# Cutting the normalisation of attention products into two pieces on VectorE, and moving the query projection one slot ahead

## The chip, the cores and the metric

One core of a Trainium2 chip. The metric is the device time of one execution in microseconds. The kernel before took 652.82 us, the median of three runs (652.71 to 653.96).

## The reference, cut to what matters

A batch of 8 images goes through two convolution blocks and then, as 256 tokens of 256 channels per image, through two attention layers with a small linear layer behind each. The change lies in the attention layers. For each of 16 heads of 16 dimensions:

```python
scores = q @ k.T / sqrt(dh) (+ bias in the first layer), masked causally
attn   = softmax(scores)
out    = (attn @ v)  -> (B, L, D)
t      = t + out @ w_out (+ b_out)
```

The softmax is not normalised where it is computed: the exponentials are multiplied with v and with a column of ones, and the product is divided by that column's result afterwards. The first attention layer (stage 0) is followed by a matrix product with ternary weights (stage 1), the second (stage 2) by a mixture of 8 experts, of which 2 count for each token (stage 3).

## The kernel before, in words

**Bodies and slots.** After the convolutions the work is 16 bodies: body 0 to 7 is stage 0 for image 0 to 7, body 8 to 15 is stage 2 for image 0 to 7. Each body starts 12 slots after the one before it (`BODY = 12`). A body is cut into pieces, each with a step; the slot of a piece is 12 times the body's number plus its step. `in_order` (L142) sorts all pieces of all bodies by slot, and each engine walks through that list in order. There are two lists: one for TensorE, and one for VectorE (DVE), ScalarE (ACT), GpSimd (POOL) and the DMA queue of SyncE (SP). Within a slot the scores and their maxima (S, MS, M) come first in the second list, then the long readings of slots before (V, PR, FF, E), then the pieces of `attention` (X, O0, O1, ON), then the pieces of `FLOW`; of those the ones of the later body come first. In any stretch of 12 slots pieces of several bodies are mixed. Below, "slot k" counts within the 12.

**The pieces, by the slot of a regular stretch in which they stand before the change.**

- S (12 per body, slots 0 to 11): a matmul of scores on TensorE; VectorE takes the negated row maximum (L1465). MS (L1474, L1475): VectorE splits a group's maxima into two bf16 parts; M (L1251): TensorE turns them, and ScalarE copies them beside the queries (L1361).
- X (12 per body, 6 slots behind S): scores again, transposed and with the maximum taken off (L1262, L1266); ScalarE takes the exponential into a ring of 9 (L1367).
- O0, O1 (L1278, L1285): products with v for the four groups of heads, pair 0 in slot 1 and pair 1 in slot 7, into PSUM bank 7.
- ON (L1476): for each pair, VectorE transposes the products (L1478, `by_token`), takes the reciprocals of the sums (L1481, `oinv`), multiplies (L1482, `attn`) and transposes back (L1486, `attnT`). Pair 0 stands in slot 2 of the next body's stretch, pair 1 in slot 8.
- PR (slot 10, L1203 with `wo`): the output projection of the body before, on TensorE; it waits for `attn_ready` of pair 1. VectorE adds the old tokens (L1495).
- LNa, LNb (stage 0 or 2, for the body two ahead: slots 3 and 5): VectorE's statistics (L1410 to L1416), GpSimd's power (L1147), VectorE's normalisation (L1421, `xn`). T (slot 6): TensorE transposes `xn` (L1187 with `fix,xn`), ScalarE copies it out (L1332). Q (slot 8) and K (slot 9): projections of the body two ahead (L1195); ScalarE writes the first bf16 part (L1346, L1349), VectorE the rest (L1431, L1434). SPLIT: GpSimd makes the second and third part, and SP stores them; in slot 9 for Q and 10 for K. LOAD (SP): slots 0 and 1 of the next stretch. V (slot 10, L1203 with `wt`), read by VectorE (L1456, L1458).
- For the layer behind the attention: LNa, LNb in slots 0 and 1, T in slot 3 (stage 1) or 2 (stage 3), FF (stage 1) or R, RT (router, stage 3), GT (slot 7), GB (slot 8: TensorE L1310, VectorE's `acc` L1538), E (8 expert products, slots 11 to 6, L1316; VectorE accumulates, L1548), CT (slot 8: transposes `acc` for the output, L1187 with `fix,acc`). GB's instruction on VectorE first waits for CT of the image before, which reads `acc`.

**Banks.** Every matmul piece but O0 and O1 takes one of 7 PSUM banks in turn (`RING = 7`), so that a piece waits on TensorE until what was 7 pieces earlier has been read out.

**Waits on VectorE's own results.** `settle` (L1394) increments `dve_step` and lets VectorE wait for it before the next instruction; ON settles the reciprocal and the product (`SETTLED`, L165).

Of the kernel before, what the change touches and what calls it, by code (L numbers as in the profile page):

```python
# [22 lines left out]
PAD = IMG + 2  # L23
HEADS, DH = 16, 16
GROUPS = 4
# [48 lines left out]
PT_RING = 9  # L74
STACKS = 3
LAG = 6
PARTS_OF_MAX = 2

Q_PARTS = (0, 0, 1, 1, 0, 2)
K_PARTS = (0, 1, 0, 1, 2, 0)  # L80
STACK = DH * len(Q_PARTS)
MAX_ROWS = PARTS_OF_MAX * HEADS // GROUPS
MAX_AT, BIAS_AT = STACK, STACK + MAX_ROWS
# [16 lines left out]
def attention():  # L100

    out = [("S", u, u) for u in range(UNITS)]
    out += [("MS", g, 3 * g + 2) for g in range(GROUPS)]
    out += [("M", g, 3 * g + 4) for g in range(GROUPS)]
    out += [("X", u, u + LAG) for u in range(UNITS)]
    for g in range(GROUPS):
        last = 3 * (g | 1) + LAG
        out += [("O0", g, last + 4), ("O1", g, last + 4)]
        if g % 2:
            out.append(("ON", g // 2, last + 5))  # L110
    return out


LONG = ("V", "PR", "FF", "E")

FLOW = {
    0: (("LNa", 0, 0, -21), ("LNb", 0, 0, -19), ("XB", 0, 0, -17), ("T", 0, 0, -18), ("Q", 0, 0, -16),
        ("SPLIT", 0, 0, -15), ("K", 0, 0, -15), ("SPLIT", 0, 1, -14), ("V", 0, 0, -14), ("LOAD", 0, 0, -12),
        ("LOAD", 0, 1, -11), ("PR", 0, 0, 22), ("LNa", 1, 0, 24), ("LNb", 1, 0, 25),
        ("T", 1, 0, 27), ("FF", 1, 0, 29)),  # L120
    2: (("LNa", 2, 0, -21), ("LNb", 2, 0, -19), ("T", 2, 0, -18), ("Q", 2, 0, -16),
        ("SPLIT", 2, 0, -15), ("K", 2, 0, -15), ("SPLIT", 2, 1, -14), ("V", 2, 0, -14), ("LOAD", 2, 0, -12),
# [39 lines left out]

JOBS = ("S", "M", "X", "T", "Q", "K", "V", "PR", "FF", "R", "GT", "GB", "E", "CT")

SETTLED = {"LNa": 2, "MS": 1, "ON": 2, "R": 1, "RT": 3, "E": 1}  # L165


def settled(piece):
    return SETTLED.get(piece[0], 0) + (piece[0] == "RT" and piece[3] == 3)


def signals(piece, bank):

    kind, n = piece[0], piece[3]
    out = []
    if kind in JOBS:
        out += [(f"bank_full{bank}", 1), (f"bank_drained{bank}", 1)]
    if kind == "O1":
        out.append((f"bank_full{PRODUCTS}", 1))
    if kind in SETTLED:  # L180
        out.append(("dve_step", settled(piece)))
    out += {"LNa": [("var_ready", 1), ("rstd_ready", 1)], "LNb": [("xn_ready", 1)], "XB": [("x_biased", 1)],
            "MS": [("max_split", 1)], "ON": [("products_taken", 1), ("attn_ready", 1)], "PAD": [("own_rows", 1), ("padded", 4), ("chosen", 1), ("chosen_spread", 16 * (STACKS - 1))], "CT": [("out_stored", 16)],
            "Q": [("first_ready0", 1)], "K": [("first_ready1", 1)],
            "SPLIT": [(f"second_ready{n}", 1), (f"third_ready{n}", 1), (f"parts_stored{n}", 16)],
            "LOAD": [(f"stack_loaded{n}", 16 * (len(Q_PARTS) + (piece[1] == 0 and n == 0)))],
            "R": [("router_shifted", 1)], "RT": {0: [("router_exp", 1)], 3: [("gates_ready", 1)]}.get(n, [])}.get(kind, [])
    return out


class Counts:


    def __init__(self):
        self.bank, self.after, self.total = {}, {}, {}
        jobs = 0
        for p in in_order("tensor"):
            if p[0] in JOBS:
                self.bank[p] = jobs % RING
                jobs += 1  # L200
            self.add(p, [(name, k) for name, k in signals(p, self.bank.get(p)) if name.startswith("bank")])
        for p in in_order("others"):
            self.add(p, [(name, k) for name, k in signals(p, self.bank.get(p)) if not name.startswith("bank")])
# [10 lines left out]
def build(nc, x_in, fix_in, fixb_in, bias_in, w0_in, w1_in, wt_in, wm_in, parts_dram, out):  # L214
    ctx = ExitStack()
    with ctx:
# [3 lines left out]
        def sem(name):  # L220
            return ctx.enter_context(nc.semaphore(name))
# [13 lines left out]
        def FB(name, lo=0, n=None):  # L235
            at, w = FIXB[name]
            return fixb[:, at + lo:at + lo + (w - lo if n is None else n)]
# [771 lines left out]
        with ExitStack() as c2:  # L1009
            def lb(name, shape, dt=F32):  # L1010
                return sb(name, shape, dt, c2)
# [10 lines left out]
            V = lb("V", [P, STACKS, 2, HEADS, SLOT])  # L1022
# [3 lines left out]
            by_token = lb("by_token", [P, 2, PIX // SLOT, SLOT])  # L1026
            chosen = lb("chosen", [P, HEADS // GROUPS], BF16)
            oinv = lb("oinv", [P, 2, PIX // SLOT])
# [9 lines left out]
            sems = {name: sem(name) for name in COUNTS.total}  # L1038
# [4 lines left out]
            def wait(eng, name, piece, less=0):  # L1043

                value = COUNTS.after.get((piece, name)) if piece else None
                if value is not None and value - less > asked.get((id(eng), name), 0):
                    asked[id(eng), name] = value - less
                    eng.wait_ge(sems[name], value - less)
# [7 lines left out]
            def full(eng, piece):  # L1056

                wait(eng, f"bank_full{bank_number(piece)}", piece)
# [26 lines left out]
            def previous(kind, stage, batch, n, by=1):  # L1085

                at = body(stage, batch) - by
                if at < 0:
                    return None
                s, b = BODIES[at]  # L1090
                return kind, s + stage % 2, b, n
# [5 lines left out]
            def earlier_unit(kind, stage, batch, n, by, per):  # L1097

                return previous(kind, stage, batch, (n - by) % per, (by - n + per - 1) // per)
# [74 lines left out]
            def tensor_piece(pe, piece):  # L1174
                kind, stage, batch, n = piece
# [23 lines left out]
                def toks(w, wstep, w_at, src, width=CH):  # L1199

                    for t in range(2):
                        for c in range(NC2):
                            mm = pe.matmul(d[:, t * width:(t + 1) * width], src[:, c, t * P:(t + 1) * P],  # L1203
                                           w[:, c * wstep + w_at:c * wstep + w_at + width],
                                           start=(c == 0), stop=(c == 1))
                    return mm
# [13 lines left out]
                if kind == "S":  # L1220
# [12 lines left out]
                    g, part = n // 3, n % 3  # L1233
# [19 lines left out]
                if kind == "X":  # L1253

                    g, part = n // 3, n % 3
# [31 lines left out]
                                       start=False, stop=True, skip_group_check=True)  # L1287
                    mm.then_inc(sems[f"bank_full{PRODUCTS}"], 1)
                if kind == "PR":
                    wait(pe, "attn_ready", ("ON", stage, batch, GROUPS // 2 - 1))  # L1290
                    if piece == ("PR", *BODIES[0], 0):
                        pe.wait_ge(wo_loaded, 16 * 2 * (HEADS // GROUPS))
                    mm = toks(wo[:, stage // 2], CH, 0, attnT)
# [95 lines left out]
            def vector_piece(dve, piece):  # L1389
                kind, stage, batch, n = piece  # L1390
# [3 lines left out]
                def settle(ins):  # L1394

                    local[0] += 1
                    ins.then_inc(sems["dve_step"], 1)
                    wait(dve, "dve_step", piece, settled(piece) - local[0])
# [39 lines left out]
                if kind == "PAD":  # L1438
                    dve.wait_ge(fixb_loaded, 16)
                    rows = slice(MAX_AT, MAX_AT + MAX_ROWS)  # L1440
                    half = MAX_ROWS // PARTS_OF_MAX
                    dve.tensor_tensor(chosen[rows, :], FB("ident", MAX_AT, half)[rows, :],
# [17 lines left out]
                if kind == "S":  # L1460
                    full(dve, piece)
                    g, part = n // 3, n % 3
# [5 lines left out]
                if kind == "MS":  # L1468
# [3 lines left out]
                    full(dve, earlier_unit("M", stage, batch, n, 2, GROUPS))  # L1472
                    first, second = (nparts[:, n % 2, :, MAX_AT + 4 * r:MAX_AT + 4 * r + 4] for r in range(PARTS_OF_MAX))
                    settle(dve.tensor_copy(first, nmax[:, par, n]))  # L1474
                    dve.tensor_tensor(second, nmax[:, par, n], first, ALU.subtract).then_inc(sems["max_split"], 1)  # L1475
                if kind == "ON":  # L1476
                    full(dve, ("O1", stage, batch, 2 * n + 1))
                    dve.transpose(by_token[:].rearrange("p g m s -> p (g m s)"), ps[:, PRODUCTS, :])\  # L1478
                       .then_inc(sems["products_taken"], 1)
                    wait(dve, "products_taken", piece)  # L1480
                    settle(dve.reciprocal(oinv[:], by_token[:, :, :, DH]))  # L1481
                    settle(dve.tensor_tensor(attn[:].rearrange("p m g d -> p g m d"), by_token[:, :, :, 0:DH],  # L1482
                                             oinv[:].unsqueeze(3).broadcast_to([P, 2, PIX // SLOT, DH]), ALU.mult))
                    if n == 0:
                        full(dve, previous("PR", stage, batch, 0))
                    dve.transpose(attnT[:, n, :], attn[:].rearrange("p m g d -> p (m g d)"))\  # L1486
                       .then_inc(sems["attn_ready"], 1)
# [11 lines left out]
                L, D, C, one, two, E = (lg[:, k] for k in range(6))  # L1499
# [211 lines left out]
```

## Time and profile before

| | us |
|---|---|
| three timed runs | 652.71, 653.96, 652.82 (median 652.82) |
| the profiled execution | 654.44 |
| its span in the trace | 652.6 |
| TensorE (matmul) busy | 571.2, 88% of the span |
| VectorE busy | 471.1, 72% |
| ScalarE busy | 300.2, 46% |

The convolutions take the first 130 us, the 16 bodies the rest. A stretch of 12 slots takes about 25.6 us while stage 0 runs and about 37.8 us in stage 2. An engine's busy time is the union of its instructions; a matmul's end is modelled, so neighbouring matmuls overlap in the rows. Behind a row, "[idle before <-releaser]" is how long the engine had stood still, and what ended that.

### The profile page before, as it was taken

How to read it: one execution, taken by the hardware profiler on the slowest of the kernel's cores; microseconds unless marked ns; L12 is line 12 of the kernel's file. 1: busy time of each engine (PE TensorE's matmuls, PEld its weight loads, DVE VectorE, ACT ScalarE, POOL GpSimd, SP SyncE). 2: the span in 40 equal slices, each digit the busy share in tenths (PEclk: the TensorE clock that was granted, in tenths of full speed). 3: DMA queues.
4: the chain of work that ended last, by engine and by line, in shares of the span. 5: the costliest groups of instructions: out<-in, count | busy, mean ns of one | idle time of the engine just before them, and what ended most of it. 6: DMA issues, size and time to landing. Idle time of an engine off the chain costs nothing.

```text
span 652.6 us, 10840 instructions
## 1 busy us (share of the span) xinstructions
PE 571.2 (88%) x3994; PEld 385.6 (59%) x4032; DVE 471.1 (72%) x1273; ACT 300.2 (46%) x472; POOL 117.5 (18%) x115
## 2 busy tenths in 40 slices
PE   9875776857988989889889897999999999999997
PEld 3743334745666757757667665657575666555443
DVE  4677858747587687786776876686868768786764
ACT  2356677626455555554545544334343434343110
POOL 2121000351213413313122031203020110000000
PEclk9996998979899999999999997999999999999999
DMA  9700000574224044053142240404113050000000
GB/s 336 256 1 1 1 0 8 136 214 119 66 85 150 27 125 125 31 145 102 46 146 74 74 146 0 146 2 127 37 53 110 16 146 1 17 5 14 17 18 16
DMA packets 40636, 51.15 MB, mean 78 GB/s; under 512 B 4180, under 2 KB 33620, under 8 KB 40276
## 3 DMA queue, kind: packets, MB, share of 16 engines
q1 hardware_dynamic: 40584, 50.46, 25.5%
q8 instruction: 32, 0.52, 0.3%
q14 instruction: 20, 0.16, 0.1%
HBM read 35.63 MB, written 14.68 MB: 77 GB/s over the span
## 4 chain that ended last, share of the span: by engine, by line
PE 50%; DVE 25%; issue 3%; DMA 2%; SPq 1%; ACT 1%; POOL 1%; DVEq 0%; ACTq 0%
PE ps L1316 13%; PE ps L1203 8%; DVE nmax L1465 7%; PE ps L1195 7%; PE ps L1278 4%; PE ps L1266 3%; PE ps L1246 3%; DVE xn L1421 2%; PE ps L1187 2%; DVE acc L1548 2%; PE ps L1262 2%; DVE stats L1410 2%; PE ps L1285 2%; PE ps L1241 2%; DVE by_token L1478 1%
## 5 line engine op out<-in xcount | busy, mean ns | idle before, releaser
L1367 ACT ACTIVATE PT<-ps 128x512 f32<-128x512 f32 x192 | 113.9, 597 | 152.0 <-PE ps L1266 150.5
L1465 DVE TENSOR_REDUCE nmax<-ps 128x2 f32<-128x512 f32 (+1 forms) x192 | 129.7, 683 | 73.3 <-PE ps L1246 70.7
L1316 PE MATMUL ps<-wm,xnT 128*128 128x512 f32 x256 | 120.2, 600 | 0.5 <-DVE acc L1548 0.5
L1361 ACT ACTIVATE QS<-ps 8x1024 bf16<-8x1024 f32 x64 | 65.0, 1016 | 28.9 <-PE ps L1251 27.9
L1266 PE MATMUL ps<-QS,KS 110*128 110x256 bf16 (+3 forms) x512 | 74.5, 247 | 0.0
L1262 PE MATMUL ps<-fixb 128*128 128x256 bf16 (+1 forms) x192 | 60.0, 313 | 16.0 <-DVE nmax L1465 11.3
L1548 DVE SCALAR_TENSOR_TENSOR acc<-ps,gate,acc 128x256 f32<-128x256 f32 x128 | 61.5, 481 | 16.6 <-PE ps L1316 14.3
L1147 POOL TENSOR_TENSOR rstd<-ve,fix 128x2 f32<-128x2 f32 x31 | 21.5, 693 | 258.4 <-DVE ve L1416 258.4
L1316 PEld LDWEIGHTS ps<-wm,xnT 128*128 128x128 f32 x256 | 44.6, 190 | 39.4 <-issue 38.0
L1195 PE MATMUL ps<-xnT,by_dim 128*128 128x256 f32 x256 | 61.0, 383 | 2.2 <-ACT xnT L1332 2.2
L1167 POOL TENSOR_TENSOR parts<-rest,fix 128x512 bf16<-128x512 f32 x30 | 38.0, 1267 | 135.0 <-DVE rest L1434 96.7
L1266 PEld LDWEIGHTS ps<-QS,KS 110*128 110x128 bf16 (+1 forms) x512 | 45.2, 98 | 12.0 <-issue 1.7
L1195 PEld LDWEIGHTS ps<-xnT,by_dim 128*128 128x128 f32 x256 | 46.3, 190 | 8.2 <-ACT xnT L1332 1.8
L1246 PE MATMUL ps<-KS,QS 110*128 110x256 bf16 (+1 forms) x256 | 50.5, 279 | 0.0
L1203 PE MATMUL ps<-wt,xnT 128*128 128x256 f32 x192 | 45.8, 381 | 0.0
L1278 PE MATMUL ps<-PT,V 128*32 128x256 f32 x512 | 41.9, 401 | 0.0
L1203 PEld LDWEIGHTS ps<-wt,xnT 128*128 128x128 f32 x192 | 34.8, 190 | 4.1
L1241 PE MATMUL ps<-fixb 128*128 128x256 bf16 x128 | 35.9, 281 | 1.3 <-DVE rest L1431 1.3
L1171 POOL TENSOR_TENSOR parts<-rest,parts 128x512 bf16<-128x512 f32 x30 | 34.7, 1156 | 2.4
L1246 PEld LDWEIGHTS ps<-KS,QS 110*128 110x128 bf16 (+1 forms) x256 | 25.8, 101 | 14.3 <-issue 8.3
L1187 PE MATMUL ps<-fix,xn 128*128 128x128 f32 x128 | 20.9, 288 | 13.0 <-DVE xn L1421 11.3
L1262 PEld LDWEIGHTS ps<-fixb 128*128 128x128 bf16 x192 | 18.8, 98 | 22.3 <-DVE nmax L1465 13.8
(217 smaller groups left out, 878.3 us busy)
## 6 DMA issues: line engine op xcount, KB each, us to landing
parts_dram<-parts SPq DMA_DIRECT2D x32, 384.0 KB, 3.1
QS<-parts_dram SPq DMA_DIRECT2D x96, 128.0 KB
KS<-parts_dram SPq DMA_DIRECT2D x96, 128.0 KB, 2.7
wt<-wt_dram SPq DMA_DIRECT2D x1, 2562.0 KB, 21.0
wm<-wm_dram SPq DMA_DIRECT2D x1, 2449.0 KB, 13.0
xc<-x_dram SPq DMA_DIRECT2D x8, 256.0 KB, 5.4
out_dram<-res SPq DMA_DIRECT2D x8, 256.0 KB, 2.1
w<-w_dram SPq DMA_DIRECT2D x1, 845.0 KB, 7.6
```

The costliest lines, as they stand in the source:

```text
L1195: mm = pe.matmul(d[:, o * PIX:(o + 1) * PIX], w[:, c, o], src[:, c, :], start=(c == 0), stop=(c == 1))
L1203: mm = pe.matmul(d[:, t * width:(t + 1) * width], src[:, c, t * P:(t + 1) * P], w[:, c * wstep + w_at:c * wstep + w_at + width], start=(c ...
L1241: pe.matmul(d.rearrange("p (j k n) -> p j k n", j=2, k=2)[:, :, 1, :], FB("ident"), FB("tri1").rearrange("p (j n) -> p j n", j=2), start=T ...
L1246: mm = pe.matmul(d[:, jj * PIX:(jj + 1) * PIX], QS[r, at, h, P:2 * P], KS[r, at, h, :], start=False, stop=(jj == 1), skip_group_check=True)
L1262: pe.matmul(d.rearrange("p (j n) -> p j n", n=width)[:, :, 0:P], FB("tri0", 0, P), FB("ident").unsqueeze(1).broadcast_to([P, len(heads), P ...
L1266: mm = pe.matmul(d[:, k * width:(k + 1) * width], KS[r, at, 4 * g + j, kt * P:(kt + 1) * P], QS[r, at, 4 * g + j, kt * P:], start=False, s ...
L1278: pe.matmul(o[32 * j:32 * j + 32, 0:PIX], V[:, at, 0, 4 * n + j, :], PT[:, pt_slot(piece, 3 * n + j // 2), (j % 2) * PIX:(j % 2 + 1) * PIX ...
L1316: mm = pe.matmul(d, normT(stage, batch)[:, c, t * P:(t + 1) * P], M("We", c * EXPERTS * CH + e * 2 * CH, 2 * CH), start=(c == 0), stop=(c ...
L1361: act.activation(QS[MAX_AT:MAX_AT + MAX_ROWS, stack(stage, batch), 4 * n:4 * n + 4, :], bank(piece)[MAX_AT:MAX_AT + MAX_ROWS, 0:PIX].unsqu ...
L1367: act.activation(PT[:, pt_slot(piece, n), :], bank(piece), ACT.Exp).then_inc(drain(piece), 1)
L1465: dve.tensor_reduce(group[:, 0, :] if part == 0 else group[:, 1, 2 * part - 2:2 * part], bank(piece).rearrange("p (j n) -> p j n", n=w_), ...
L1548: op = dve.scalar_tensor_tensor(acc[:, t, :], bank(piece)[:, k * CH:(k + 1) * CH], gate[:, par, t, 2 * e + k:2 * e + k + 1], acc[:, t, :], ...
```

## The change

ON keeps the first transposition and the reciprocals. The product and the transposition back become a piece AT of their own, two slots behind ON for pair 0 (slot 2 to 4) and one slot behind it for pair 1 (slot 8 to 9). The reciprocals now count on a semaphore of their own, on which AT waits. Q goes from slot 8 to 7, its SPLIT from 9 to 8; K stays.

```diff
+TURN_BACK = (7, 6)
...
         if g % 2:
-            out.append(("ON", g // 2, last + 5))
+            out += [("ON", g // 2, last + 5), ("AT", g // 2, last + TURN_BACK[g // 2])]
...
-    0: (... ("Q", 0, 0, -16),
-        ("SPLIT", 0, 0, -15), ("K", 0, 0, -15), ...
+    0: (... ("Q", 0, 0, -17),
+        ("SPLIT", 0, 0, -16), ("K", 0, 0, -15), ...
...
-    2: (... ("Q", 2, 0, -16),
-        ("SPLIT", 2, 0, -15), ("K", 2, 0, -15), ...
+    2: (... ("Q", 2, 0, -17),
+        ("SPLIT", 2, 0, -16), ("K", 2, 0, -15), ...
...
-SETTLED = {"LNa": 2, "MS": 1, "ON": 2, "R": 1, "RT": 3, "E": 1}
+SETTLED = {"LNa": 2, "MS": 1, "AT": 1, "R": 1, "RT": 3, "E": 1}
...
-            "ON": [("products_taken", 1), ("attn_ready", 1)]
+            "ON": [("products_taken", 1), ("inverse_ready", 1)], "AT": [("attn_ready", 1)]
...
                 if kind == "PR":
-                    wait(pe, "attn_ready", ("ON", stage, batch, GROUPS // 2 - 1))
+                    wait(pe, "attn_ready", ("AT", stage, batch, GROUPS // 2 - 1))
...
                     wait(dve, "products_taken", piece)
-                    settle(dve.reciprocal(oinv[:], by_token[:, :, :, DH]))
+                    dve.reciprocal(oinv[:], by_token[:, :, :, DH]).then_inc(sems["inverse_ready"], 1)
+                if kind == "AT":
+                    wait(dve, "inverse_ready", ("ON", stage, batch, n))
                     settle(dve.tensor_tensor(attn[:].rearrange("p m g d -> p g m d"), by_token[:, :, :, 0:DH],
```

By the sorting rule VectorE's order in a regular stretch becomes: slot 2: S, MS, ON (pair 0); slot 3: S, LNa; slot 4: S, AT (pair 0); slot 5: S, MS, LNb; slot 7: S, Q; slot 8: S, MS, ON (pair 1), GB where there is one; slot 9: S, AT (pair 1), K; slot 10: S. TensorE's order becomes, from slot 7: S, M, X, O0, O1, Q, GT, S, X, GB, CT, S, X, K, S, M, X, V, PR. Bodies 14 and 15 have no Q, K and V beside them (there is no body two ahead), and behind body 15's scores there is no S either: VectorE's order at the end is ON (pair 1), GB, AT (pair 1).

## Rows read from the trace of the kernel before

**Rows 1.** By stretch: length, busy PE, PEld, DVE, ACT, POOL; granted clock, DMA, GB/s.

```profile
240.60:266.21 25.61, 22.78 (x207) 17.27 (x209) 19.32 (x54) 13.94 (x23) 7.50 (x7) 1.00 0.32 95
...
391.50:396.10 4.60, 0.76 (x8) 0.32 (x5) 4.08 (x19) 2.81 (x5) 0.69 (x1) 0.95 0.00 1
396.10:402.50 6.40, 6.35 (x49) 4.08 (x50) 2.41 (x9) 2.59 (x4) 0.00 (x0) 0.50 0.00 0
```

**Rows 2.** What TensorE waited for, 170 to 380 us: total, times, longest.

```profile
PE ps L1262 <- DVE nmax L1465: 11.3, 8, 1.4
PE ps L1187 <- DVE xn L1421: 2.5, 8, 0.3
```

**Rows 3.** The chain that ended last, one regular stretch: start, us, what.

```profile
253.22 0.70 DVE nmax L1465
...
266.21 0.66 PE ps L1187 x4
...
278.83 0.70 DVE nmax L1465
```

**Rows 4.** Timeline of VectorE around ON of pair 0: start, us, instruction.

```profile
209.68 0.25 DVE L1481 RECIPROCAL oinv<-by_token 128x16 f32<-128x16 f32 x1
209.96 0.42 DVE L1482 TENSOR_TENSOR attn<-by_token,oinv 128x256 f32<-128x256 f32 x1
210.42 0.45 DVE L1486 STREAM_TRANSPOSE attnT<-attn 128x256 f32<-128x256 f32 x1
210.79 0.65 DVE L1465 TENSOR_REDUCE nmax<-ps 128x4 f32<-128x512 f32 x1
...
212.50 1.28 DVE L1465 TENSOR_REDUCE nmax<-ps 128x2 f32<-128x512 f32 x2
```

**Rows 5.** Timeline of TensorE: T of body 3 and of body 15.

```profile
160.99 1.09 PE L1187 MATMUL ps<-fix,xn 128*128 128x128 f32 x4 [2.85 <-DVE xn L1421]
...
510.43 0.63 PE L1187 MATMUL ps<-fix,xn 128*128 128x128 f32 x4 [0.62 <-DVE xn L1421]
```

**Rows 6.** Timeline, slots 8 to 10 of one stretch: S, Q, its readings, PR.

```profile
217.79 0.28 PE L1241 MATMUL ps<-fixb 128*128 128x256 bf16 x1
...
218.33 0.69 DVE L1465 TENSOR_REDUCE nmax<-ps 128x2 f32<-128x512 f32 x1 [1.60 <-PE ps L1246]
...
218.57 1.95 PE L1195 MATMUL ps<-xnT,by_dim 128*128 128x256 f32 x8
...
220.56 0.84 ACT L1346 ACTIVATE parts<-ps,qk_bias 128x256 bf16<-128x256 f32 x2 [1.19 <-PE ps L1195]
...
221.43 0.88 DVE L1431 SCALAR_TENSOR_TENSOR rest<-ps,qk_bias,parts 128x256 f32<-128x256 f32 x2
...
225.36 1.89 PE L1203 MATMUL ps<-wo,attnT 128*128 128x256 f32 x8
```

**Rows 7.** Timeline of TensorE: expert products, right behind O1 and behind T.

```profile
419.67 1.98 PE L1316 MATMUL ps<-wm,xnT 128*128 128x512 f32 x4
...
422.71 1.88 PE L1316 MATMUL ps<-wm,xnT 128*128 128x512 f32 x4
```

**Rows 8.** Timeline: ON of pair 1 of body 13, GB, PR.

```profile
553.82 0.25 DVE L1481 RECIPROCAL oinv<-by_token 128x16 f32<-128x16 f32 x1
...
554.94 0.65 DVE L1538 TENSOR_TENSOR acc<-ps,xt 128x512 f32<-128x512 f32 x1
...
555.64 1.99 PE L1203 MATMUL ps<-wo,attnT 128*128 128x256 f32 x8 [0.44 <-DVE acc L1538]
```

**Rows 9.** Timeline of the end: ON of pair 1 of body 15, GB, PR.

```profile
611.50 0.25 DVE L1481 RECIPROCAL oinv<-by_token 128x16 f32<-128x16 f32 x1
...
613.27 0.69 DVE L1538 TENSOR_TENSOR acc<-ps,xt 128x512 f32<-128x512 f32 x1 [0.57 <-PE ps L1187]
...
613.00 1.89 PE L1203 MATMUL ps<-wo,attnT 128*128 128x256 f32 x8
```

**Rows 10.** The chain that ended last, behind PR of body 15.

```profile
614.89 1.73 PE ps L1316 x4
```

More of the change, by code:

```diff
@@ L116 @@
 FLOW = {
-    0: (("LNa", 0, 0, -21), ("LNb", 0, 0, -19), ("XB", 0, 0, -17), ("T", 0, 0, -18), ("Q", 0, 0, -16),
-        ("SPLIT", 0, 0, -15), ("K", 0, 0, -15), ("SPLIT", 0, 1, -14), ("V", 0, 0, -14), ("LOAD", 0, 0, -12),
+    0: (("LNa", 0, 0, -21), ("LNb", 0, 0, -19), ("XB", 0, 0, -17), ("T", 0, 0, -18), ("Q", 0, 0, -17),
+        ("SPLIT", 0, 0, -16), ("K", 0, 0, -15), ("SPLIT", 0, 1, -14), ("V", 0, 0, -14), ("LOAD", 0, 0, -12),
         ("LOAD", 0, 1, -11), ("PR", 0, 0, 22), ("LNa", 1, 0, 24), ("LNb", 1, 0, 25),
         ("T", 1, 0, 27), ("FF", 1, 0, 29)),
-    2: (("LNa", 2, 0, -21), ("LNb", 2, 0, -19), ("T", 2, 0, -18), ("Q", 2, 0, -16),
-        ("SPLIT", 2, 0, -15), ("K", 2, 0, -15), ("SPLIT", 2, 1, -14), ("V", 2, 0, -14), ("LOAD", 2, 0, -12),
+    2: (("LNa", 2, 0, -21), ("LNb", 2, 0, -19), ("T", 2, 0, -18), ("Q", 2, 0, -17),
+        ("SPLIT", 2, 0, -16), ("K", 2, 0, -15), ("SPLIT", 2, 1, -14), ("V", 2, 0, -14), ("LOAD", 2, 0, -12),
         ("LOAD", 2, 1, -11), ("PR", 2, 0, 22),
@@ L182, in signals @@
     out += {"LNa": [("var_ready", 1), ("rstd_ready", 1)], "LNb": [("xn_ready", 1)], "XB": [("x_biased", 1)],
-            "MS": [("max_split", 1)], "ON": [("products_taken", 1), ("attn_ready", 1)], "PAD": [("own_rows", 1), ("padded", 4), ("chosen", 1), ("chosen_spread", 16 * (STACKS - 1))], "CT": [("out_stored", 16)],
+            "MS": [("max_split", 1)], "ON": [("products_taken", 1), ("inverse_ready", 1)], "AT": [("attn_ready", 1)], "PAD": [("own_rows", 1), ("padded", 4), ("chosen", 1), ("chosen_spread", 16 * (STACKS - 1))], "CT": [("out_stored", 16)],
             "Q": [("first_ready0", 1)], "K": [("first_ready1", 1)],
```

## The prediction

> **What bounds the kernel now.** I read the busy time by stretch first. In a regular stretch of stage 0 TensorE works 22.78 of 25.61 us and VectorE 19.32 [rows 1], so neither fills the stretch, and the loss must be turns of waiting. The waits of TensorE name two on VectorE that come back in all 8 bodies of that time: X (L1262) waits 1.41 us for the reading of a score bank, and T (L1187) waits 0.32 us for `xn` [rows 2]. They are not worth their length. The chain of waits shows why: from 253.22 to 266.21 it runs on VectorE alone, from the maximum of slot 11 through ON of pair 0 to LNb of slot 5; then T starts and it runs on TensorE to 278.83, where VectorE's next maximum of slot 11 begins [rows 3]. A stretch is thus VectorE's work from slot 11 to LNb plus TensorE's work from T to slot 11. Only what shortens or crosses one of these two halves counts. X's 1.41 us lie inside VectorE's half: what TensorE saves there it waits again at T.
>
> **Part 1: AT of pair 0 goes from slot 2 to 4.** LNb stands in slot 5, so product and transposition (0.42 and 0.45 us, [rows 4]) stay in VectorE's half, ahead of LNb. The maximum of slot 3 is read some 0.9 us earlier and X's wait falls from 1.41 to about 0.5, but T's grows by as much. What remains is the seams. Now the product starts 0.03 us after the reciprocals end (209.93 to 209.96), since it waits for them; the maximum behind the transposition starts 0.08 before that ends (210.87, 210.79); two maxima in a row take 1.28 us though one takes 0.65 to 0.69, which is again about 0.08 of overlap [rows 4]. The three seams sum to +0.03 - 0.08 - 0.08 = -0.13 us now; afterwards all three are free of a wait, 3 x -0.08 = -0.24. That is 0.11 us less in each stretch whose T waits for LNb. T waits from body 3 (2.85 us) to body 15 (0.62 us) [rows 5], 13 times in all: 13 x 0.11 = **1.4 us saved**. Bounds: 0, if the overlap is only how the records end, and 2.6 (0.2 in each, twice what I read).
>
> The Trainium skill (VectorE: DVE Perf Modes, "The DRAIN you can't avoid") says that a semaphore between chained VectorE operations costs nothing extra. By that the 1.4 us fall away and the sum is +3.1 in place of +1.7; the rows differ, with 0.03 after a wait against -0.08 without, so I go by them.
>
> **Part 2: Q one slot ahead, AT of pair 1 one behind, bodies with Q, K and V beside them.** These lie in TensorE's half. Q's matmuls take the place of S at 217.79 instead of 218.57 [rows 6]; the sum of TensorE's work is the same but for the joints. An expert product right behind O1 takes 1.98 us, behind a fp32 piece 1.88 [rows 7], so that joint costs 0.10; Q behind X, a bf16 piece, takes 1.95 against 1.89 of PR, whose matmuls are as large and follow V's [rows 6], so the joint that goes away cost 0.06. That is 0.04 us more in each of the 9 stretches where Q now stands behind O1 and no GT stood there before: **+0.4 us**, bounds 0 and +0.9 (0.1 each).
>
> VectorE's order becomes S, Q's rest, S, MS, transposition and reciprocals, S, AT, K's rest. The rest waits for ScalarE's copies, which wait for Q: they start 0.04 us after Q ends (220.52, 220.56 [rows 6]), so now near 219.8, and the rest near 220.7. From S to the end of the rest VectorE ran from 218.33 to 222.31, 3.98 us; the same work with one more maximum (0.68) in front of AT now runs from 220.7 to about 225.2 less the seams, 225.1. PR starts at 225.36 [rows 6], so it does not wait, with 0.2 us to spare. VectorE's own lateness ends before slot 11's maximum, for which it waited anyhow. GpSimd's split of Q and SP's store move with Q to an earlier time; SP takes stores and loads in order, and the loads stand behind K's store, which does not move; the loads are a whole stretch ahead of their use. Cost 0; without that slack each tenth of lateness of PR costs 9 x 0.1 us in stage 0.
>
> **Part 3: bodies 13 and 14.** No Q, K and V stand in their stretches, so PR comes early: it waits 0.44 us for the bank that GB's addition frees (554.94 + 0.65), and would start right after the transposition otherwise. Now GB follows the reciprocals (end 554.07): 553.99 to 554.64; the maximum of slot 9, 0.68, to 555.24; product to 555.59, transposition from 555.62 to 556.07, PR at 556.11 against 555.64 [rows 8]. From there TensorE works without a gap to the next such wait. One more body (14) has the same 0.44: 2 x 0.47 = **+0.9 us**, bounds 0.8 and 1.0.
>
> **Part 4: the end.** Behind body 15 no maximum of slot 9 stands between, but GB does: its addition waits for CT's transpositions on TensorE and starts at 613.27 [rows 9]. Before, ON was through by then, the reciprocals having ended at 611.75, and PR began at 613.00. Now AT stands behind that addition: product from 613.88 to 614.31, transposition from 614.35 to 614.80, PR at 614.85. Taking PR's own start and the 0.1 us that it overlapped CT, that is **+1.8 us**, bounds 1.7 and 1.95. Nothing behind takes it up: in the chain PR is followed on TensorE by the first expert product of image 6 [rows 10], and VectorE's accumulation of that stands ahead of body 15's LNa, from which all the rest hangs.
>
> **Sum:** -1.4 + 0.4 + 0.9 + 1.8 = +1.7 us. The profiled execution took 654.44 us (its span 652.6) and would take 656.1; it lies 1.62 above the median of the runs, from which I count: 652.82 + 1.7 = **654.5 us**, +0.26%. A measurement can tell about 0.2% (1.3 us) from no change, so the forecast lies just beyond. Bounds together: -2.6 + 0 + 0.8 + 1.7 = -0.1, and 0 + 0.9 + 1.0 + 1.95 = +3.9.
>
> **Rivals.**
>
> 1. *The seams give nothing* (the rule above): +3.1, 655.9 us. For it: the overlap is the records' end, not a start of work. Against: starts do follow each other faster. Chance 0.18.
> 2. *The seams give twice as much* (0.2 per stretch): +3.1 - 2.6, 653.3 us, no change. Chance 0.18. *The end is hidden* (+1.7 - 1.8): 652.7, no change; against it stands the unbroken chain. Chance 0.05.
> 3. *X's wait is the real bound*, the case of not slower: if T's matmuls were not held by LNb but came when TensorE gets there, the 0.87 us that leave the way of slot 3's maximum would count in the 8 bodies of stage 0, 7.0 us less: 652.82 + 3.1 - 7.0 = 648.9 us. It decides where T's wait on `xn` is zero; it is 0.32 in each of the 8 bodies [rows 2], and the order keeps AT ahead of LNb. Chance 0.05.
> 4. *The clock.* Near 396 us TensorE worked 0.76 of 4.60 us, and after that the granted clock was 0.50 (the 1.2 GHz level) for 6.4 us of nearly full work [rows 1]. Splitting ON moves idle time about inside that stretch: 3.2 us gained if it now keeps 2.4 GHz (651.3, chance 0.06), 3.2 us lost if another stretch falls, such as the one before body 3's T, whose wait of 2.85 [rows 5] grows by 0.9 (657.7, chance 0.03).
> 5. *PR or M late in part 2*: the spare 0.2 us is worked out from five steps; off by 0.6 the other way, 9 x 0.4 = 3.6 more: 658.1. Chance 0.05.
>
> **How the numbers follow.** The forecast has 0.40, of which 0.30 lie beyond +0.2% and 0.10 within. Slower: 0.30 + 0.18 + 0.05 + 0.03 = 0.56. Same: 0.10 + 0.18 + 0.05 = 0.33. Faster: 0.05 + 0.06 = 0.11. The range 652.2 to 656.6 holds the forecast, rivals 1 and 2 with the bounds of the sum, and leaves out rivals 3 to 5, 0.19. Slower cases alone lie from 654.2 to 656.6.
>
> **What would show it.** Right: in stage 0 X's wait on the maximum falls to about 0.5 us and T's on `xn` rises to about 1.2, a stretch stays within 25.4 to 25.6 us; PR of bodies 13 and 14 waits about 0.9 us; PR of body 15 starts about 1.7 us after CT, with TensorE idle between. Wrong: a stretch of stage 0 shorter by 0.3 us or more, T without a wait, PR waiting on AT in stage 0, or the end no longer from PR of body 15 than before.

## The result and the profile after

The changed kernel took 655.58 us (median of 7 runs, 654.99 to 658.25) against 652.86 us for the kernel before (7 runs, 652.11 to 654.95): ratio 1.0039, interval 1.0022 to 1.0057, about 2.7 us slower. The profiled execution took 655.45 us, with a span of 653.6.

The totals of the page tell nothing: TensorE 572.4 us busy (571.2 before), VectorE 471.2 (471.1). So I cut each stretch at the two points of the prediction: the maximum of slot 11 and T. What lies from the maximum to T's start I call VectorE's half, what lies from T to the next maximum of slot 11 TensorE's half. Busy time by stretch, both halves of one stretch of stage 0, then of one of stage 2; columns are the stretch, its length, busy PE, PEld (TensorE's weight loads), DVE, ACT, POOL, the granted clock, DMA share, GB/s. The kernel before:

```profile
253.22:266.21 12.99, 10.21 (x105) 7.07 (x104) 11.87 (x38) 6.99 (x11) 1.39 (x2) 1.00 0.52 156
266.21:278.83 12.62, 12.57 (x103) 10.19 (x105) 7.44 (x16) 6.94 (x12) 6.12 (x5) 1.00 0.11 33
450.67:472.61 21.94, 21.03 (x131) 11.73 (x132) 18.84 (x60) 7.50 (x12) 1.38 (x2) 1.00 0.31 91
472.61:488.49 15.88, 15.83 (x117) 12.33 (x119) 10.03 (x25) 7.38 (x13) 4.85 (x4) 1.00 0.14 43
```

And the changed kernel:

```profile
251.35:264.14 12.79, 10.20 (x104) 7.07 (x104) 11.71 (x38) 7.30 (x11) 2.25 (x3) 1.00 0.54 159
264.14:277.03 12.89, 12.83 (x103) 10.09 (x105) 7.51 (x16) 6.63 (x11) 5.27 (x5) 1.00 0.11 32
448.10:470.04 21.94, 20.83 (x132) 11.70 (x132) 18.85 (x60) 7.51 (x12) 1.38 (x2) 1.00 0.32 91
470.04:486.20 16.16, 16.05 (x117) 12.36 (x119) 10.20 (x25) 7.26 (x12) 4.87 (x4) 1.00 0.14 42
```

In these rows VectorE's half got 0.20 shorter in stage 0 and nothing in stage 2; TensorE's half got 0.27 and 0.28 longer. The waits of TensorE between 170 and 380 us moved as forecast against [rows 2]: X's fell, T's rose.

```profile
PE ps L1188 <- DVE xn L1422: 8.8, 8, 1.1
PE ps L1263 <- DVE nmax L1466: 3.5, 8, 0.4
```

Bodies 13 and 14 and the end answer to [rows 8, 9]. Timeline of TensorE and VectorE: PR of body 13, and then GB's addition, AT and PR of body 15.

```profile
554.17 1.97 PE L1204 MATMUL ps<-wo,attnT 128*128 128x256 f32 x8 [0.96 <-DVE attnT L1489]
...
612.26 0.69 DVE L1541 TENSOR_TENSOR acc<-ps,xt 128x512 f32<-128x512 f32 x1 [1.51 <-PE ps L1188]
612.87 0.42 DVE L1485 TENSOR_TENSOR attn<-by_token,oinv 128x256 f32<-128x256 f32 x1
613.32 0.45 DVE L1489 STREAM_TRANSPOSE attnT<-attn 128x256 f32<-128x256 f32 x1
...
613.91 1.97 PE L1204 MATMUL ps<-wo,attnT 128*128 128x256 f32 x8 [1.76 <-DVE attnT L1489]
```

PR waits 0.96 us where it waited 0.44, and at the end VectorE stands idle 1.51 us for CT, and AT behind it keeps TensorE idle 1.76 us.

**What lengthened TensorE's half in stage 0** is in slot 8. Timeline of VectorE, then of GpSimd and TensorE, changed kernel:

```profile
218.46 0.88 DVE L1432 SCALAR_TENSOR_TENSOR rest<-ps,qk_bias,parts 128x256 f32<-128x256 f32 x2 [3.96 <-ACT parts L1347]
219.25 0.68 DVE L1466 TENSOR_REDUCE nmax<-ps 128x2 f32<-128x512 f32 x1
220.13 0.57 DVE L1475 CAST nparts<-nmax 128x8 bf16<-128x8 f32 x1 [0.20 <-DVE nmax L1466]
220.74 0.17 DVE L1476 TENSOR_TENSOR nparts<-nmax,nparts 128x8 bf16<-128x8 f32 x1
...
222.73 0.45 DVE L1489 STREAM_TRANSPOSE attnT<-attn 128x256 f32<-128x256 f32 x1
...
219.41 1.26 POOL L1168 TENSOR_TENSOR parts<-rest,fix 128x512 bf16<-128x512 f32 x1 [5.35 <-DVE rest L1432]
...
221.05 0.27 PE L1252 MATMUL ps<-fixb,nparts 128*128 128x128 bf16 x2
...
221.49 1.89 PE L1204 MATMUL ps<-wt,xnT 128*128 128x256 f32 x8
223.32 1.97 PE L1204 MATMUL ps<-wo,attnT 128*128 128x256 f32 x8
225.12 0.27 PE L1242 MATMUL ps<-fixb 128*128 128x256 bf16 x1
```

The cast of MS takes 0.57 us and ends at 220.70, 0.03 after GpSimd's first instruction of Q's split (220.67), which now runs beside it. Over the whole kernel the 64 casts took 11.0 us before and 16.7 after:

```profile
L1474 DVE CAST nparts<-nmax 128x8 bf16<-128x8 f32 x64 | 11.0, 172 | 10.6 <-DVE nmax L1465 6.4
L1475 DVE CAST nparts<-nmax 128x8 bf16<-128x8 f32 x64 | 16.7, 261 | 11.2 <-DVE nmax L1466 6.8 <-ACT PT L1368 0.6
```

M starts 0.06 us late (0.28 behind the scores ahead of it at 220.77, where it was 0.22). PR starts 1.83 behind V (at 221.49), where it was 1.73: AT's transposition ends at 223.18, and PR follows it by 0.14, as it does at the end of the program, where it waits for AT openly (613.77, 613.91). PR then takes 1.80 of TensorE's time to the next piece (at 225.12) for 1.73. Together 0.23 us.

**What lengthened it in stage 2** is on ScalarE. Timeline of ScalarE and TensorE, changed kernel:

```profile
476.55 0.60 ACT L1350 ACTIVATE parts<-ps 128x512 bf16<-128x512 f32 x1 [2.06 <-PE ps L1196]
477.04 0.38 ACT L1374 ACTIVATE gateT<-ps 128x256 f32<-128x256 f32 x1
...
477.12 0.39 PE L1267 MATMUL ps<-QS,KS 104*128 104x128 bf16 x4
477.57 1.10 PE L1311 MATMUL ps<-wm,gateT 128*128 128x256 f32 x4
```

Q now stands ahead of GT, so ScalarE copies Q first and the transposed gates second (ending at 477.42). GB on TensorE starts 0.45 us behind the start of X's last matmuls; before, the piece behind the same X followed 0.23 after (477.92 to 478.15), and GB took 0.86 of TensorE's time, now 0.94. Together 0.3 us.

### The profile page after: what moved, and what is told of

It reads as the page before. It is cut to its first block, busy times and chain, and to the rows that moved or that the text cites. A ratio compares the mean times of both kernels' runs of the same rounds, so it can differ in the third digit from the quotient of the medians.

```text
span 653.6 us, 10846 instructions
## 1 busy us (share of the span) xinstructions
PE 572.4 (88%) x3994; PEld 385.5 (59%) x4032; DVE 471.2 (72%) x1273; ACT 299.7 (46%) x472; POOL 117.9 (18%) x115
## 4 chain that ended last, share of the span: by engine, by line
PE 50%; DVE 25%; issue 3%; DMA 1%; SPq 1%; ACT 1%; POOL 1%; DVEq 0%; ACTq 0%
PE ps L1317 13%; PE ps L1204 8%; PE ps L1196 7%; DVE nmax L1466 7%; PE ps L1279 4%; PE ps L1267 3%; PE ps L1247 3%; DVE xn L1422 2%; DVE acc L1551 2%; PE ps L1188 2%; PE ps L1263 2%; DVE stats L1411 2%; PE ps L1286 2%; DVE by_token L1479 1%; PE ps L1242 1%
## 5 line engine op out<-in xcount | busy, mean ns | idle before, releaser
L1196 PE MATMUL ps<-xnT,by_dim 128*128 128x256 f32 x256 | 63.3, 393 | 2.2 <-ACT xnT L1333 2.2
L1432 DVE SCALAR_TENSOR_TENSOR rest<-ps,qk_bias,parts 128x256 f32<-128x256 f32 x32 | 13.7, 471 | 29.4 <-ACT parts L1347 29.4
```

The lines of the kernel that those rows point to most:

```text
L1196: mm = pe.matmul(d[:, o * PIX:(o + 1) * PIX], w[:, c, o], src[:, c, :], start=(c == 0), stop=(c == 1))
```

## The experiments

All halves below are read from the timeline in the same way (start of the maximum of slot 11 to start of T, and on to the next one); "4 + 4" are the first four and the next four of the eight stretches of stage 0 that begin between some 172 and 360 us. The columns are medians, in us; stretches with a spell at half the clock are left out of the halves, and where the three of stage 2 differ their median stands. The ratios below are to runs of the kernel before that were taken beside each experiment (medians 652.34 of 29 runs for e1 to e4, 653.02 of 9 for e5 to e7, 652.43 of 7 for e9 and e10). e6, e7 and e9 ran once: their halves are read, their times carry no interval.

| kernel | time (runs) | VectorE's half, stage 0 | TensorE's half, 4 + 4 | VectorE's, TensorE's half, stage 2 | PR waits: bodies 13, 14; 15 |
|---|---|---|---|---|---|
| before | 652.86 (7) | 12.98 | 12.63 + 12.63 | 21.94, 15.88 | 0.44; 0 |
| changed | 655.58 (7) | 12.80 | 12.89 + 12.66 | 21.93, 16.17 | 0.96; 1.76 |
| e1 | 653.68 (12) | 12.79 | 12.63 + 12.63 | 21.93, 15.88 | 0.97; 1.76 |
| e2 | 656.98 (6) | 12.98 | 13.00 + 12.66 | 21.94, 16.23 | 0.44; 0 |
| e3 | 655.35 (12) | 12.79 | 12.99 + 12.66 | 21.92, 16.23 | 0.44; 0 |
| e4 | 655.85 (12) | 12.78 | 12.89 + 12.66 | 21.92, 16.17 | 0.96; 1.76 |
| e5 | 639.74 (5) | 12.00 | 12.63 + 12.63 | 21.14, 15.88 | 0.44; 0.11 |
| e6 | 656.07 (1) | 12.79 | 12.90 + 12.66 | 21.92, 16.17 | 0.97; 1.75 |
| e7 | 654.81 (1) | 12.79 | 12.90 + 12.62 | 21.92, 15.88 | 0.97; 1.76 |
| e9 | 653.47 (1) | 12.79 | 12.66 + 12.66 | 21.93, 16.17 | 0.97; 1.76 |
| e10 | 644.70 (4) | 12.00 | 12.90 + 12.66 | 21.14, 16.17 | 0.97; 1.76 |

**e1: Q back, the pieces of ON kept apart.** The changed kernel with

```diff
-("Q", 0, 0, -17), ("SPLIT", 0, 0, -16)   (and the same in stage 2)
+("Q", 0, 0, -16), ("SPLIT", 0, 0, -15)
```

> The changed kernel with Q and its split back in their old slots; AT stays apart from ON. Theory A (Q's move has costs of its own: GpSimd's split of Q stretches VectorE's cast in MS from 0.17 to 0.57 us, which makes PR late in the stretches where both Q's reading and PR belong to stage 0, and in stage 2 the copy of the turned gates waits behind Q's copy on ScalarE): the casts are all 0.17 us again, TensorE's half of a stretch of stage 0 goes from 12.89 back to about 12.63 and in stage 2 from 16.17 to about 15.88; VectorE's half stays at 12.80. Time 2.0 to 2.4 us under the changed kernel, about 653.4, +0.6 over the kernel before. Rival B (PR is late because AT stands behind one more maximum, whatever Q does): TensorE's half stays near 12.85 in stage 0 and the time falls by 1 us or less, to about 654.8.

Measured: 653.68 us (651.71 to 654.48), ratio to before 1.0018, interval 0.9998 to 1.0037. VectorE's half keeps its gain, TensorE's half loses all that it had grown by, and bodies 13 and 14 and the end keep their price. So the gain belongs to AT of pair 0, the growth of TensorE's half to Q, in both stages.

**e2: Q ahead alone.** The changed kernel with `TURN_BACK = (5, 5)`, which puts AT right behind ON again.

> Q and its split one slot ahead as in the change, but AT right behind ON in the same slot, so that product and turning back stand where they stood before. Theory A: VectorE's half is 12.98 as before, the cast of MS in slot 8 takes about 0.57 us, TensorE's half in stage 0 grows by 0.05 to 0.1 only (AT is early, PR is not late), in stage 2 by 0.29 in each of 3 to 4 stretches; bodies 13, 14 and the end as before. Time +1.5 to +2 over the kernel before, about 654.5. Rival B: TensorE's half as before everywhere, +0.4 at most, 653.3.

Measured: 656.98 us (655.31 to 659.65), ratio 1.0081, interval 1.0052 to 1.011: a miss by 2.5 us. Bodies 13 and 14 and the end are as before, as expected. But TensorE's half grew by 0.37 in stage 0, where 0.05 to 0.1 was expected and the change itself has 0.27. So AT of pair 1 behind the next maximum did not cause the lateness; it softens it, and what PR waits for in its place shows at e3. The profiled execution has two spells in stage 0 at a granted clock of 0.50 (the 1.2 GHz level), each of which makes its stretch's VectorE half 1.2 us longer (14.18 where the others take 12.98). By the halves e2 lies 2.8 us above the kernel before, by the medians of the same batch 4.6; where the other runs had their spells is not on record, so the rest stays open. Busy time by stretch, e2:

```profile
264.96:268.37 3.41, 3.41 (x10) 2.43 (x9) 2.59 (x10) 0.60 (x1) 1.19 (x2) 0.50 0.16 53
343.47:346.88 3.41, 3.41 (x10) 2.32 (x9) 2.50 (x9) 0.52 (x1) 0.69 (x1) 0.50 0.01 5
```

**e3: only pair 1 together again.** `TURN_BACK = (7, 5)`, Q ahead as in the change.

> The change, but AT of pair 1 in the slot of ON (0 slots apart in place of 1); AT of pair 0 still two behind, Q still one ahead. Theory A: PR of bodies 13 and 14 waits 0.44 us again and not 0.96, PR of body 15 follows CT without a wait, and PR in stage 0 is no longer late: 0.98 + 1.9 + 0.7 = 3.6 us less than the changed kernel, about 652.0, that is 0.9 below the kernel before. Rival (the end is hidden and the loss is all Q's): within 0.7 us of the changed kernel.

Measured: 655.35 us (651.1 to 656.37), ratio 1.0034, interval 1.0014 to 1.0055: a miss by 3.4 us. The price of bodies 13 and 14 and of the end is gone (2.9 us), as expected. But TensorE's half did not fall; it is longer than in the change, 4 x 0.10 in stage 0 and 0.3 in all in stage 2, which gives back some 0.7: near 653.4 by the parts. Timeline of VectorE and TensorE, e3:

```profile
221.17 0.45 DVE L1489 STREAM_TRANSPOSE attnT<-attn 128x256 f32<-128x256 f32 x1
221.53 0.65 DVE L1466 TENSOR_REDUCE nmax<-ps 128x4 f32<-128x512 f32 x1
...
222.24 1.99 PE L1204 MATMUL ps<-wo,attnT 128*128 128x256 f32 x8
```

AT is through at 221.62, yet PR starts only at 222.24, 0.06 behind the end of the maximum of slot 9 (222.18). PR takes the bank of the scores of slot 9, which stand seven pieces ahead of it on TensorE; in e2 and e3 their maximum stands behind AT, in the change ahead of it. So with AT early PR waits for the bank, with AT late for AT.

The runs spread over 5 us and go by their mean granted clock: the three at 0.974 to 0.976 took 651.1 to 652.6 us, the other nine, at 0.964 to 0.971, 654.0 to 656.4. Why one execution has more time at half the clock than another stays open.

**e4: another form of the slow cast.** The cast written as a product with ones:

```diff
-settle(dve.tensor_copy(first, nmax[:, par, n]))
+settle(dve.tensor_tensor(first, nmax[:, par, n], F("ones", 0, 8)..., ALU.mult))
```

> The changed kernel with the first instruction of MS (the cast of 8 numbers per row from fp32 to bf16) written as a product with ones; the result is the same. Theory A: if it is the cast alone that GpSimd's running instruction holds up, this product takes about 0.17 us everywhere, PR and M are no longer late, and TensorE's half of the stretches of bodies 1 to 4 falls from 12.89 to about 12.68: 0.8 us less in all, about 654.8. Rival D (any small VectorE instruction is held up while GpSimd works, or the cast waits for something else): the product takes about 0.57 in slot 8 as the cast did, no change of the time.

Measured: 655.85 us (653.71 to 657.97). The product is held as long. Timeline of VectorE and GpSimd, e4:

```profile
218.75 0.57 DVE L1475 TENSOR_TENSOR nparts<-nmax,fix 128x8 bf16<-128x8 f32 x1 [0.20 <-DVE nmax L1466]
...
218.03 1.27 POOL L1168 TENSOR_TENSOR parts<-rest,fix 128x512 bf16<-128x512 f32 x1 [5.36 <-DVE rest L1432]
```

It ends at 219.32, GpSimd's instruction at 219.30. So rival D of this expectation holds: the hold does not hang on the instruction being a cast.

**e6 and e9: GpSimd's split behind the cast.** One wait more ahead of the split; e6 named the body before the right one (`- 3`), e9 the right one:

```diff
+if n == 0 and body(stage, batch) >= 3:
+    wait(eng, "max_split", ("MS", *BODIES[body(stage, batch) - 2], 2))
```

> The changed kernel, but GpSimd begins its split of Q only when VectorE has split the maxima of group 2 in the same slot. Theory C (VectorE's cast of slot 8 is held by GpSimd's instruction beside it, and this is what makes M late): all casts of nmax take 0.17 us again, and TensorE's half falls from 12.89 to 12.65 to 12.75 us in the four stretches of stage 0 where it grew. Rival (Q's rest ahead of S and MS makes VectorE late, whatever the cast takes): casts 0.17 us, half still 12.8 to 12.95 us. In the three stretches of stage 2 no difference by either, unless the cast is what costs there: 16.17 us.

> The changed kernel, but GpSimd begins its split of Q only when VectorE has split the maxima of group 2 of the body whose slots run (the run before it, meant for the same, waited on the body before that one, so GpSimd still began beside the cast: cast 0.57 us, half 12.89, as in the changed kernel). Theory C (the cast is held by GpSimd's instruction beside it, which makes M late): the casts of slot 8 take 0.17 us again, and TensorE's half falls from 12.89 to 12.65 to 12.75 us in the four stretches of stage 0 where it grew. Rival (Q's rest ahead of S and MS makes VectorE late, whatever the cast takes): casts 0.17 us, half still 12.8 to 12.95 us.

Measured: in e6 the wait had long been met, GpSimd still began first, and nothing changed: 656.07 us, cast 0.57. In e9 the split waits. Timeline of VectorE and GpSimd, e9:

```profile
218.38 0.17 DVE L1477 CAST nparts<-nmax 128x8 bf16<-128x8 f32 x1 [0.20 <-DVE nmax L1468]
218.58 0.17 DVE L1478 TENSOR_TENSOR nparts<-nmax,nparts 128x8 bf16<-128x8 f32 x1
...
218.92 1.27 POOL L1170 TENSOR_TENSOR parts<-rest,fix 128x512 bf16<-128x512 f32 x1 [6.62 <-DVE nparts L1478]
```

The cast is back at 0.17 us and TensorE's half at 12.66 in all four stretches, 0.23 less; stage 2 does not move. Same order of work on VectorE, only GpSimd begins later: the cast's hold is the cause in stage 0. The one time, 653.47 us, is 2.1 below the change, more than the 0.9 that this accounts for. What is left lies in the convolutions, where the edit changes nothing: the first T starts at 110.83 us here and at 112.20 in the profile of the change.

**e7: Q back in stage 2 alone.** The edit of e1 in stage 2 only.

> The changed kernel, but in stage 2 the query projection and its split stand in their old slots; stage 0 as changed. Theory E (in stage 2 the cost is ScalarE's copy of Q, now ahead of the copy of the gates that GB waits for): TensorE's half of the three stretches of stage 2 falls from 16.17 back to 15.85 to 15.9 us, the stretches of stage 0 stay at 12.89. Rival (AT of pair 1 behind GB's addition costs there): it stays over 16.1 us.

Measured: 654.81 us; TensorE's half in stage 2 is 15.88 again in all three stretches, with AT of pair 1 still one slot behind ON. So AT behind GB's addition is out as a cause there, and Q's move is the cause. It moved both the split and ScalarE's copy; in e9 the cast is free and these stretches stay at 16.17, so the split's hold of the cast is out too. What remains, beside the joint of some 0.03, is the copy, and in the change GB starts 0.15 behind its end (477.42, 477.57).

**e5 and e10: AT of pair 0 behind LNb.** e5 is e1 with `TURN_BACK = (9, 5)`, e10 the changed kernel with `TURN_BACK = (9, 6)`.

> The query projection in its old slot, AT of pair 1 back in the slot of ON, AT of pair 0 two slots further than in the changed kernel, behind LNb of the image two ahead. Theory A (a stretch is VectorE's work from slot 11 to LNb plus TensorE's from T to slot 11; the change kept AT of pair 0 inside the first half, so only the seams counted): product and transposition, 0.42 + 0.45 us, leave VectorE's half in the 13 stretches whose T waits; the half falls from 12.98 to between 11.9 and 12.1 us, TensorE's half stays at 12.6 to 12.8, time 640 to 643 us. Theory B (the 0.5 us that X still waits, or another reading of a bank, takes T's place): VectorE's half falls by less than 0.4 us or TensorE's half grows by as much, time over 648 us.

> The changed kernel with one number more: AT of pair 0 two slots further, behind LNb, the rest as changed. The run with both other parts undone as well gained 13.9 us against the same kernel with AT ahead of LNb, of which 2.8 are bodies 13, 14 and the end (the medians 639.74 and 653.68). Theory A (the two parts add up): VectorE's half 11.9 to 12.1 us, TensorE's half as in the changed kernel (12.89, 12.66), time 655.6 less 11.1, 643 to 646 us. Rival (with VectorE's half shorter, the late cast and Q's copy are hidden or grow): TensorE's half moves by over 0.1 us, time under 642 or over 647 us.

Measured: e5 639.74 us (638.92 to 642.06), ratio 0.9808, interval 0.9784 to 0.9833; e10 644.70 us (643.85 to 645.64), ratio 0.9878, interval 0.9856 to 0.9899. Busy time by stretch, the two halves in e5:

```profile
247.87:259.86 11.99, 10.27 (x105) 7.07 (x103) 10.94 (x36) 6.96 (x11) 1.39 (x2) 1.00 0.58 170
259.86:272.50 12.64, 12.62 (x104) 10.20 (x105) 8.32 (x18) 6.97 (x12) 6.12 (x5) 1.00 0.12 33
```

VectorE's half has 36 instructions where it had 38 and is 0.98 shorter in the table; the two that left now run beside TensorE's half, which stays as it was (12.64 in this row, 12.63 in the table). In timeline and waits nothing has taken T's place: T waits 0.3 us on `xn`, as in [rows 2], and X 0.4 on the bank. Against the changed kernel e10 has VectorE's half 0.80 shorter in stage 0, with Q's and AT's prices unchanged; 13 x 0.80 is 10.4 of the 10.9 us between the medians, so the parts add up. e5 beats both kernels.

## Why the prediction was right, and where it was wrong

**The frame held.** A stretch is VectorE's work from slot 11 to LNb plus TensorE's from T on. X's wait fell to 0.44 where 0.5 was forecast, T's rose to 1.1 where 1.2 was; none of X's 0.97 counted. Two signs did not come out: the first four stretches took 25.69 us, outside the 25.4 to 25.6, and PR waited on AT in stage 0, which had been named as a sign of being wrong and belongs to part 2. Rival 3 (X's wait is the bound) is out, and e5 shows what would have had to move: not the distance of AT to ON, but its side of LNb.

**Part 1, seams: mis-sized both ways.** Forecast 0.11 us in each of 13 stretches. In stage 0 it was 0.18 (0.19 in several). Timeline of VectorE, changed kernel, beside [rows 4]:

```profile
259.01 0.25 DVE L1482 RECIPROCAL oinv<-by_token 128x16 f32<-128x16 f32 x1
259.18 0.63 DVE L1466 TENSOR_REDUCE nmax<-ps 128x4 f32<-128x512 f32 x1
...
260.86 0.68 DVE L1466 TENSOR_REDUCE nmax<-ps 128x2 f32<-128x512 f32 x1
261.46 0.41 DVE L1485 TENSOR_TENSOR attn<-by_token,oinv 128x256 f32<-128x256 f32 x1
261.91 0.45 DVE L1489 STREAM_TRANSPOSE attnT<-attn 128x256 f32<-128x256 f32 x1
262.28 0.65 DVE L1466 TENSOR_REDUCE nmax<-ps 128x2 f32<-128x512 f32 x1
```

The three seams are as worked out: the maximum starts 0.08 before the reciprocals end, the product 0.08 before that maximum's end, the next maximum 0.08 before the transposition's end. From the reciprocals' start to the next instruction it is now 0.17 us where it was 0.28. The rest, some 0.07, is hundredths in the instructions themselves (the maximum 0.63 and the product 0.41, for 0.65 and 0.42; the maximum ahead of LNb's cast 0.65 for 0.68). In the three stretches of stage 2 it was 0, where the step assumed the same: there the maximum of slot 3 starts at 460.31, and the scores that it reads end on TensorE at 460.28, behind an expert product. The maximum comes 0.27 behind the start of the reciprocals there, not 0.17. Timeline of TensorE and VectorE:

```profile
459.89 0.39 PE L1239 MATMUL ps<-KS,QS 96*128 96x128 bf16 x4
...
460.31 0.69 DVE L1466 TENSOR_REDUCE nmax<-ps 128x4 f32<-128x512 f32 x1
```

In all the gain was about 10 x 0.18 = 1.8 us, not 1.4; rival 1 (seams give nothing) is out. The rule of the Trainium skill (VectorE: DVE Perf Modes, "The DRAIN you can't avoid"), by which a semaphore in a chain costs nothing extra, does not agree with these rows: 0.28 with the wait against 0.17 without, though the instruction behind is another one (the product, and the maximum in its place).

**Part 2, the step that failed.** The joint was right: Q behind O1 costs 0.03 to 0.04 (12.66 against 12.63 in the second four stretches, and in the first four once e9 frees the cast). Two sentences were wrong. "GpSimd's split of Q and SP's store move with Q to an earlier time", priced "Cost 0", looked at what waits for the split, and not at what runs beside it: the cast is held 0.40 us. The spare of PR had been worked out as 0.2 with every instruction at its old duration. The working is loose: 220.7 + 3.98 + 0.68 is 225.36 and not 225.2, and it allows 0.04 from AT's transposition to PR, where the runs show 0.14. Its result is near all the same: in e9, with the cast free, AT ends at 221.02 and PR starts at 221.41, a spare of 0.39 less 0.14, 0.25. The hold of 0.40 makes PR 0.15 late; measured are 0.16 (M's 0.06 and PR's 0.10), and the 0.07 that PR then takes longer make up the 0.23. It costs only in the four stretches whose Q and K are of stage 0 (a fifth holds a half-clock spell and can't be told), where the reading of Q is two instructions, 0.88 us together; in the next four it is one of 0.69 and the spare covers the held cast:

```profile
346.19 0.69 DVE L1435 TENSOR_TENSOR rest<-ps,parts 128x512 f32<-128x512 f32 x1 [3.72 <-ACT parts L1350]
...
347.68 0.57 DVE L1475 CAST nparts<-nmax 128x8 bf16<-128x8 f32 x1 [0.20 <-DVE nmax L1466]
```

That is rival 5, at a quarter of its price. And the 9 stretches "where Q now stands behind O1 and no GT stood there before" leave out those of stage 2, at no cost: moving Q past GT reorders ScalarE's queue too, 3 x 0.29 us. Part 2 was 4 x 0.27 + 4 x 0.04 + 3 x 0.29 = 2.1 us, not 0.4, without the two stretches that hold half-clock spells.

**Parts 3 and 4 were right.** Bodies 13 and 14: 0.49 each for a forecast 0.47 (AT's transposition was through a little sooner than worked out, and PR followed it by 0.14, not 0.04). The end: PR started 25.21 us behind the last maximum of slot 11 instead of 23.29, 1.92 for 1.8, and nothing behind took it up. e3 takes both away by `TURN_BACK` alone.

**Sum.** The parts as measured give -1.8 + 2.1 + 1.0 + 1.9 = +3.2 us; the medians say +2.7, with an interval of 1.4 to 3.7; forecast was +1.7. The two profiled spans differ by 1.0 only, since the half-clock spells lie otherwise in them: the half-stretch behind 160 us takes 15.41 us before and 14.28 after, and what lies ahead of the first maximum of slot 11 is 0.8 shorter after. So the direction and the size were right for the larger part by parts 3 and 4, which came out as worked out. Parts 1 and 2 were both off, by 0.4 and 1.7 us, on opposite sides: that they partly cancel is luck. It is chance too that rival 1's 655.9 us lies nearest to the result; its seams that give nothing were not found.

## What to carry to other kernels

A split that moved work within the half-stretch that sets the end gained its seams and some hundredths, nothing else; ask first which piece ends that half (here LNb), and move work past it: the same two instructions, two slots further, took 11 us off the changed kernel (e10). When a piece moves, follow it on every engine that it uses, ScalarE and GpSimd too, and ask for each both who queues behind it and what now runs at the same time. Look at the ends of the chain by themselves, where a fixed delay has no other work to cover it.

## What the runs showed of the hardware

While GpSimd runs an elementwise instruction of 1.27 us on 128x512, some of VectorE's instructions that start beside it end only behind it: the cast of 128x8 (0.57 us for 0.17, 0.84 at most, in the kernel before never above 0.17) and the product of two such operands (e4: 0.57) some 0.03 us behind, and in e1 the product of AT (128x256), which there runs beside the split, 1.11 us for 0.41, 0.27 behind (222.86, 222.59). Others keep their time: in e9 the reciprocals (0.25 at 219.41) and a maximum from PSUM (0.63 at 219.58), both beside the split's first instruction, and in e1 AT's transposition beside the second. Timeline of VectorE and GpSimd, e1:

```profile
221.75 1.11 DVE L1485 TENSOR_TENSOR attn<-by_token,oinv 128x256 f32<-128x256 f32 x1
222.90 0.45 DVE L1489 STREAM_TRANSPOSE attnT<-attn 128x256 f32<-128x256 f32 x1
...
221.32 1.27 POOL L1168 TENSOR_TENSOR parts<-rest,fix 128x512 bf16<-128x512 f32 x1 [6.10 <-DVE rest L1432]
222.66 1.22 POOL L1172 TENSOR_TENSOR parts<-rest,parts 128x512 bf16<-128x512 f32 x1
```

The Trainium skill (GPSIMD Engine Reference, "Key points") says that GpSimd shares its SBUF interfaces with VectorE and contends with VectorE's instructions that have two SBUF inputs or run in a 2-port perf mode. These rows agree for the two products; the cast has one input, and no run here shows in which mode it ran.
